# Giving the second level of the gated expert sum from VectorE to TensorE, with a shorter end of the last stage

## The chip, the cores and the metric

The kernel runs on one core of a Trainium2 chip. Its time is the device time of one execution, in microseconds. Before the change it is 437.8 us, the median of 3 runs (437.61 to 437.95).

## What is computed

The input is x with 32 sequences of 128 positions and 128 features, all in f32, and a context of the same shape. There are two gated residual blocks:

```
x = x + tanh(g_xattn) * attention16(layernorm(x), ctx, ctx)
x = x + tanh(g_ffn)   * block(layernorm(x))

def block(x):
    attn_out = causal_attention16(rope(x), rope(x), x) @ out_proj
    x1    = layernorm(x + attn_out) * ln1_w + ln1_b
    gates = softmax(x1 @ gate_w.T + gate_b)            # 8 experts
    top_gates, top = top_k(gates, 2)
    y[e]  = x1 @ expert_w[e].T + expert_b[e]           # all 8 are computed
    moe   = sum over the two chosen experts of top_gates * y[e]
    return layernorm(x1 + moe) * ln2_w + ln2_b
```

## The kernel before

Two sequences form a pair (g, 0 to 15; `LAST` is 15, `G` is 2). The first three quarters of the time are the two attentions, in slots of one tile. What this case is about is the last phase, which turns each pair's attention output into the result. It begins in the last attention slots (the `early` functions) and then runs in bodies s = 3, 4, ... (`z_steps`), one for each pair. Every engine has its own program, written out by hand, and its order is the order of the code: an engine that waits for a semaphore holds up all behind it. A body works on several pairs at once, in stages that are one body apart.

TensorE, body s, in this order: the second four experts of pair s-2 (`experts(..., 1)`, L927), transposes of pair s's attention output (L878), the product of the gates with the expert biases of pair s-3 (L946), the transpose of the gates of pair s-2 (L936), transposes of the normalised rows of pair s-1 (L901), `gated_sum` of pair s-3 (L951), the output projection of pair s (L890), the gate logits of pair s-1 (L913), and the first four experts of pair s-1 (`experts(..., 0)`, L927). An f32 product is two instructions, each with its weight load.

The four experts of the first half (in `s_bank`) are weighted and added up by VectorE from PSUM: eight instructions `z_acc` (L1232), four experts for two sequences. The four of the second half (in `st_bank`) are weighted by ScalarE into the tile `z_gated` (L1070; for the last pair L1081). VectorE adds these four to two (`gated_pairs`, L1241, 128x512) and the two to one (`gated_sum`, L1248, 128x256, tile `z_gated_sum`). TensorE multiplies the result by the identity matrix `idf`, so that it is accumulated in PSUM on the gated biases; one VectorE addition (`experts_add`, L1258) then joins it with `z_acc`. For pair 15 there are no VectorE levels: TensorE sums the four weighted experts by four identity products (`last_gated_sum`, L959), and then adds the biases (L962).

VectorE, body s: `gated_pairs` of pair s-3; the negated mean of pair s-4; `gating` of pair s-2 (L1203 to L1217: top two, sum, reciprocal, gates), with `gated_sum` of pair s-3 inside it; the accumulations of pair s-2; the attention addition of pair s (L1145, which waits for the projection); `experts_add` of pair s-3 (L1258); statistics and moments of both (L1152, L1158, L1266, L1272).

The first experts of a pair are not begun before all eight accumulations of the pair ahead have read the same banks (`pe.wait_ge(z_acc, g * ACC)`).

In the last two bodies there is no new pair. At the very end VectorE has additions, statistics and moments of pairs 14 and 15, then `weigh` (L1289) for both and `close` (L1298) for both. The factor 1/sqrt(var + eps) is made by GpSimd in two instructions (L796 and the power, L798), for pair 14 and then for pair 15; each `close` waits for its own. ScalarE issues the two last stores (L1131).

Of the kernel before, what the change touches and what calls it, by code (L numbers as in the profile page):

```python
# [53 lines left out]
def gated_block_kernel(nc, x, ctx_in, g_x, g_f, wq_t, wk_t, wv_t, wo_t, bq, bk, bv, bo,  # L54
# [3 lines left out]
    with es:  # L58
# [736 lines left out]
        def rstd_of(pool, v_in, v_eps, r_out, semaphore, k):  # L795
            pool.tensor_scalar(v_eps, v_in, 1.0, EPS, ALU.mult, ALU.add).then_inc(semaphore, 1)  # L796
            pool.wait_ge(semaphore, k + 1)
            pool.tensor_tensor(r_out, v_eps, mhalf[:, :], ALU.pow).then_inc(semaphore, 1)  # L798
# [14 lines left out]
        zst2 = two("z_stats2_", [P, G, 6]); zmv2 = two("z_mv2_", [P, G, 2]); zve2 = two("z_ve2_", [P, G])  # L813
        zrs2 = two("z_rstd2_", [P, G]); znb2 = two("z_offset2_", [P, G]); zy = two("z_y2", [P, G, P]); zyw = sb("z_yw", [P, G, P]); zyc = two("z_yc", [P, G, P])
        zsum = two("z_x1_moe", [P, G, P]); zyg = sb("z_gated", [P, G, HALF, P]); zyp = sb("z_gated_pairs", [P, G, HALF // 2, P]); zyq = sb("z_gated_sum", [P, G, P]); zo = [sb(f"z_o{i}", [P, G, P]) for i in range(4)]
# [6 lines left out]
        z_gtc = sem("z_gates_t_copied"); z_y = [sem(f"z_experts{k}") for k in range(2)]; z_yg = sem("z_experts_gated"); z_yp = sem("z_gated_pairs_summed"); z_yq = sem("z_gated_summed"); z_yb = sem("z_expert_bias")  # L822
# [43 lines left out]
        def z_pe(pe):  # L866
# [50 lines left out]
            def experts(g, gc, k):  # L917
                i = gc % 2
                if gc == 0:
                    pe.wait_ge(ex, LAST_TILE if k else LAST_TILE - 2)  # L920
                if gc >= 1:
                    if k == 0:
                        pe.wait_ge(z_acc, g * ACC)
                for b in range(G):
                    if gc >= 1 and k == 1:
                        pe.wait_ge(z_yg, (g - 1) * G + b + 1)
                    ins = pe.matmul(e_bank[b][k][:, :], zx1t[i][:, b * P:(b + 1) * P],  # L927
                                    ewt[:, k * 512:(k + 1) * 512], start=True, stop=True)
                ins.then_inc(z_y[k], 1)
# [18 lines left out]
            def gated_sum(g, gc):  # L948
                dst = u_bank[1][:, 0:W]
                pe.wait_ge(z_yq, g + 1)  # L950
                pe.matmul(dst.rearrange("q (b d) -> q b d", b=G), idf[:, :], zyq[:, :, :],  # L951
                          start=False, stop=True).then_inc(z_yb, 1)

            def last_gated_sum(g, gc):
                dst = t_bank[:, 0:W]
                pe.wait_ge(z_x1c, GROUPS)
                for e in range(HALF):
                    pe.wait_ge(z_yg, g * G + e + 1)
                    pe.matmul(dst.rearrange("q (b d) -> q b d", b=G), idf[:, :], zyg[:, :, e, :],  # L959
                              start=e == 0, stop=False)  # L960
                pe.wait_ge(z_gtc, g + 1)
                pe.matmul(dst, zgt[gc % 2][:, :], ebs[:, :], start=False, stop=True).then_inc(z_yb, 1)  # L962
# [54 lines left out]
        def z_act(act):  # L1017
# [56 lines left out]
            def gate_last_experts(g, gc):  # L1074
                i = gc % 2
                act.wait_ge(z_gate, (g + 1) * GATE)
                act.wait_ge(z_y[1], g + 1)
                act.wait_ge(z_yp, g)
                for e in range(HALF):
                    for b in range(G):  # L1080
                        ins = act.activation(zyg[:, b, e, :], e_bank[b][1][:, e * P:(e + 1) * P], ACT.Copy,  # L1081
                                             scale=zg[i][:, b, HALF + e:HALF + e + 1])
                    ins.then_inc(z_yg, 1)
# [54 lines left out]
        def z_dve(dve):  # L1138
# [57 lines left out]
            def gating(g, gc, second_level=None):  # L1196
# [15 lines left out]
                if second_level is not None:  # L1212
                    gated_sum(*second_level)
# [6 lines left out]
            def experts(g, gc):  # L1220
                i = gc % 2
                k = g * ACC
                dve.wait_ge(z_x1, (g + 1) * 2)
                dve.wait_ge(z_gate, (g + 1) * GATE)
                dve.wait_ge(z_y[0], g + 1)
                if gc >= 2:
                    dve.wait_ge(z_all, (g - 2) * ALL + 1)
                for e in range(HALF):
                    for b in range(G):
                        if e >= 1:  # L1230
                            dve.wait_ge(z_acc, k + (e - 1) * G + b + 1)
                        dve.scalar_tensor_tensor(  # L1232
                            out=zacc[i][e % 2][:, b, :], in0=e_bank[b][0][:, e * P:(e + 1) * P],
                            scalar=zg[i][:, b, e:e + 1], in1=zacc[i][(e + 1) % 2][:, b, :] if e else zx1[i][:, b, :],
                            op0=ALU.mult, op1=ALU.add).then_inc(z_acc, 1)

            def gated_pairs(g, gc):
                dve.wait_ge(z_yg, (g + 1) * G)
                if gc >= 1:
                    dve.wait_ge(z_yq, g)  # L1240
                dve.tensor_tensor(zyp[:, :, :, :], zyg[:, :, 0:HALF // 2, :], zyg[:, :, HALF // 2:HALF, :],  # L1241
                                  ALU.add).then_inc(z_yp, 1)

            def gated_sum(g, gc):
                dve.wait_ge(z_yp, g + 1)
                if gc >= 1:
                    dve.wait_ge(z_yb, g)
                dve.tensor_tensor(zyq[:, :, :], zyp[:, :, 0, :], zyp[:, :, 1, :], ALU.add).then_inc(z_yq, 1)  # L1248

            def experts_add(g, gc):  # L1250
# [6 lines left out]
                dve.wait_ge(z_acc, (g + 1) * ACC)  # L1257
# [21 lines left out]
            def all_experts(g, gc):  # L1279
                experts_add(g, gc)  # L1280
                experts_stats(g, gc)
                experts_moments(g, gc)
                experts_minus_mean(g, gc)

# [7 lines left out]
            def close(g):  # L1292
                i = g % 2
                dve.wait_ge(z_rs2, (LAST - 1) * 3 + (i + 1) * 2)
# [6 lines left out]
            def body(s, c):  # L1301
                if in_z(c, 2) and s - 2 < LAST:
# [4 lines left out]
                    gating(s - 2, c - 2, (s - 3, c - 3) if in_z(c, 3) else None)  # L1307
                if s - 2 == LAST:
                    gating(s - 2, c - 2)
                    gated_pairs(s - 3, c - 3)  # L1310
                    gated_sum(s - 3, c - 3)
# [12 lines left out]
                else:  # L1324
                    if s - 1 == LAST:
                        shift_logits(s - 1, c - 1)
                    if s - 3 == LAST - 2:
                        all_experts(s - 3, c - 3)
# [31 lines left out]
        def z_pool(pool):  # L1360
# [203 lines left out]
```

## Time and profile before

| | |
|---|---|
| median of 3 runs | 437.8 us |
| the profiled execution, its own time | 437.07 us |
| its span, first to last instruction | 435.3 us |
| TensorE matmul busy in the span | 383.0 us (88%) |
| VectorE busy | 368.9 us (85%) |
| ScalarE busy | 288.6 us (66%) |
| GpSimd busy | 314.9 us (72%) |
| granted TensorE clock, mean | 0.994 |

The profile is of one execution. Times in it count from the first instruction. PE is TensorE's matmuls, PEld its weight loads, DVE VectorE, ACT ScalarE, POOL GpSimd. A timeline row joins neighbours of one line: its length runs from the first start to the last end. A matmul's end is modelled, and two that follow each other overlap in the rows, so their distance is read from start to start.

### The profile page before, as it was taken

How to read it: one execution, taken by the hardware profiler on the slowest of the kernel's cores; microseconds unless marked ns; L12 is line 12 of the kernel's file. 1: busy time of each engine (PE TensorE's matmuls, PEld its weight loads, DVE VectorE, ACT ScalarE, POOL GpSimd, SP SyncE). 2: the span in 40 equal slices, each digit the busy share in tenths (PEclk: the TensorE clock that was granted, in tenths of full speed). 3: DMA queues.
4: the chain of work that ended last, by engine and by line, in shares of the span. 5: the costliest groups of instructions: out<-in, count | busy, mean ns of one | idle time of the engine just before them, and what ended most of it. 6: DMA issues, size and time to landing. Idle time of an engine off the chain costs nothing.

```text
span 435.3 us, 17717 instructions
## 1 busy us (share of the span) xinstructions
PE 383.0 (88%) x6538; PEld 232.0 (53%) x6538; DVE 368.9 (85%) x1218; ACT 288.6 (66%) x728; POOL 314.9 (72%) x712
## 2 busy tenths in 40 slices
PE   0368888898888899999999999999999999999993
PEld 0134544454444556666666666666664655555542
DVE  6588999999998787788888788778867999999996
ACT  1126767767776666666666666667774888888872
POOL 4456757766778988888888888885241478778774
PEclk9999999999999999999999999999999999999997
DMA  6855686585554333344334344344000000000001
GB/s 163 195 158 159 175 206 166 154 186 150 130 150 110 103 100 100 99 107 112 102 102 109 102 119 119 105 110 113 12 8 1 2 14 25 25 27 13 25 26 49
DMA packets 88037, 42.76 MB, mean 98 GB/s; under 512 B 16000, under 2 KB 87824, under 8 KB 87952
## 3 DMA queue, kind: packets, MB, share of 16 engines
q1 hardware_dynamic: 80864, 39.59, 34.4%
q10 hardware_dynamic: 7088, 2.04, 2.0%
q8 instruction: 53, 0.87, 0.9%
q14 instruction: 32, 0.26, 0.2%
HBM read 5.69 MB, written 2.10 MB: 18 GB/s over the span
## 4 chain that ended last, share of the span: by engine, by line
PE 29%; DVE 21%; issue 4%; ACT 2%; POOL 1%; POOLq 0%; DVEq 0%; ACTq 0%
PE u_bank L499 7%; DVE z_acc L1232 5%; PE s_bank L421 5%; PE s_bank L434 4%; DVE r L697 2%; PE t_bank L413 2%; DVE z_gated_pairs L1241 2%; PE t_bank L407 2%; PE u_bank L514 1%; DVE z_stats L1266 1%; ACT part L577 1%; PE s_bank L927 1%; DVE z_stats L1152 1%; DVE z_h L1145 1%; PE st_bank L927 1%
## 5 line engine op out<-in xcount | busy, mean ns | idle before, releaser
L716 DVE TENSOR_REDUCE nm<-s_bank 128x4 f32<-128x512 f32 x256 | 171.5, 682 | 35.9 <-PE s_bank L434 33.6
L599 ACT ACTIVATE pt<-st_bank 128x512 f32<-128x512 f32 x250 | 147.5, 602 | 73.8 <-PE st_bank L434 51.4
L434 PE MATMUL s_bank<-qk 64*64 64x128 bf16 (+1 forms) x1584 | 103.7, 220 | 12.0 <-DVE nm L716 5.5
L499 PE MATMUL u_bank<-pt,vaug 128*32 128x128 f32 x2048 | 108.2, 286 | 1.7
L434 PE MATMUL st_bank<-qk 64*64 64x128 bf16 (+1 forms) x1540 | 98.3, 218 | 0.1
L434 PEld LDWEIGHTS s_bank<-qk 64*64 64x64 bf16 (+1 forms) x1584 | 73.8, 104 | 35.9 <-issue 18.7
L434 PEld LDWEIGHTS st_bank<-qk 64*64 64x64 bf16 (+1 forms) x1540 | 69.2, 103 | 0.3 <-issue 0.3
L499 PEld LDWEIGHTS u_bank<-pt,vaug 128*32 128x32 f32 x2048 | 41.2, 108 | 27.5 <-issue 5.2
L421 PE MATMUL s_bank<-mqk,idb 64*64 64x256 bf16 x256 | 38.3, 292 | 0.5 <-ACT pt L599 0.4
L327 POOL TENSOR_TENSOR part<-r,part 128x512 bf16<-128x512 f32 x32 | 37.1, 1158 | 1.4
L421 PE MATMUL st_bank<-mkq,idb 64*64 64x256 bf16 x244 | 35.7, 293 | 0.0
L606 ACT ACTIVATE mts<-m_bank 128x128 bf16<-128x128 bf16 x63 | 17.5, 278 | 24.5 <-PE m_bank L509 24.5
L338 POOL TENSOR_SCALAR mst<-nm 128x16 bf16<-128x16 f32 x64 | 13.1, 205 | 27.7 <-DVE nm L716 27.7
L927 PE MATMUL s_bank<-ewt,z_x_t 128*128 128x512 f32 x64 | 31.7, 618 | 1.0 <-DVE z_acc L1232 0.4
L514 PE MATMUL u_bank<-idf,us 128*128 128x128 f32 x128 | 28.0, 300 | 5.2 <-ACT us L615 4.9
L1070 ACT ACTIVATE z_gated<-st_bank,z_gates 128x128 f32<-128x128 f32 x120 | 32.4, 382 | 0.0
L927 PE MATMUL st_bank<-ewt,z_x_t 128*128 128x512 f32 x64 | 30.2, 594 | 0.0
L322 POOL TENSOR_SCALAR part<-r 128x512 bf16<-128x512 f32 x32 | 19.8, 617 | 10.8 <-DVE r L692 6.3
L421 PEld LDWEIGHTS s_bank<-mqk,idb 64*64 64x64 bf16 x256 | 14.4, 103 | 24.3 <-issue 14.0
L796 POOL TENSOR_SCALAR z_ve<-z_mv 128x2 f32<-128x2 f32 x32 | 6.4, 201 | 28.3 <-DVE z_mv L1158 25.5
L1232 DVE SCALAR_TENSOR_TENSOR z_acc<-s_bank,z_gates,z_acc 128x128 f32<-128x128 f32 x96 | 26.1, 342 | 0.0
L280 POOL TENSOR_TENSOR rstd<-ve,mhalf 128x2 f32<-128x2 f32 x32 | 22.6, 708 | 2.7
(138 smaller groups left out, 826.3 us busy)
## 6 DMA issues: line engine op xcount, KB each, us to landing
qk<-part SPq DMA_DIRECT2D x221, 128.0 KB, 2.7
x_all<-x SPq DMA_DIRECT2D x16, 128.0 KB, 2.7
qk<-qrow SPq DMA_DIRECT2D x32, 64.0 KB, 2.2
c_all<-ctx_in SPq DMA_DIRECT2D x14, 128.0 KB, 2.8
out<-z_o SPq DMA_DIRECT2D x14, 128.0 KB, 1.8
qk<-mts ACTq DMA_DIRECT2D x34, 32.0 KB, 2.7
qk<-mts SPq DMA_DIRECT2D x30, 32.0 KB, 2.1
ewt<-exp_t SPq DMA_DIRECT2D x1, 512.0 KB
```

Source lines behind the costliest of these rows:

```text
L280: pool.tensor_tensor(rstd[u % 2][:, :], ve[u % 2][:, :], mhalf[:, :], ALU.pow).then_inc(rstd_s, 1)
L322: pool.tensor_scalar(part[u % 2][:, 1:2 * PARTS:PARTS, :], r32[:, :].rearrange("c (o t) -> c o t", o=2), 1.0, 0.0, ALU.mult, ALU.add).then ...
L327: pool.tensor_tensor(part[u % 2][:, 2:2 * PARTS:PARTS, :], r32[:, :].rearrange("c (o t) -> c o t", o=2), part[u % 2][:, 1:2 * PARTS:PARTS, ...
L421: pe.matmul(to, idb[rows, rows], mask[rows, rows].unsqueeze(1).broadcast_to([64, HEADS, 64]), start=True, stop=False, skip_group_check=True)
L434: ins = pe.matmul(to[outs, :], fixed[:, outs], moving, start=not masked, stop=True, skip_group_check=masked)
L499: ins = pe.matmul(u_bank[b][32 * j:32 * j + 32, r * P:(r + 1) * P], v, pt[m % 4][:, j, :], start=half == 0, stop=half == 1, skip_group_che ...
L514: ins = pe.transpose(u_bank[q % 2][:, W + r * P:W + (r + 1) * P], us[q % 2][:, r * P:(r + 1) * P], idf[:, :])
L599: act.activation(pt[m % 4][:, :, :].rearrange("k j q -> k (j q)"), transposed_bank(m)[:, :], ACT.Exp).then_inc(ex, 1)
L716: dve.tensor_reduce(nm[q % 2][:, first:first + HEADS], s_bank[n % 2][:, :].rearrange("q (j k) -> q j k", j=HEADS), AX_X, ALU.max, negate=T ...
L927: ins = pe.matmul(e_bank[b][k][:, :], zx1t[i][:, b * P:(b + 1) * P], ewt[:, k * 512:(k + 1) * 512], start=True, stop=True)
L1070: ins = act.activation(zyg[:, b, e, :], e_bank[b][1][:, e * P:(e + 1) * P], ACT.Copy, scale=zg[i][:, b, HALF + e:HALF + e + 1])
L1232: dve.scalar_tensor_tensor(out=zacc[i][e % 2][:, b, :], in0=e_bank[b][0][:, e * P:(e + 1) * P], scalar=zg[i][:, b, e:e + 1], in1=zacc[i][( ...
```

## The change

The second level of the gated sum leaves VectorE. TensorE takes the two halves of `z_gated_pairs` with two identity products, both accumulated on the biases. `gated_pairs` now waits for that product (`z_yb`), since it is what frees its tile.

The wait in front of the first experts is split by sequence: the products of sequence b wait for the accumulation of sequence b alone.

For pair 15, ScalarE weights two of the second four experts and TensorE sums these two. VectorE accumulates the other two itself, straight from PSUM, after ScalarE has read the bank; it has twelve accumulations in that body and no longer eight.

The moments of pair 13 move into the gating of pair 15, and their negated mean behind it. The factors of pairs 14 and 15 are made together, by one pair of GpSimd instructions over 128x4, and both `close` wait for them.

```diff
-        def rstd_of(pool, v_in, v_eps, r_out, semaphore, k):
+        def rstd_of(pool, v_in, v_eps, r_out, semaphore, k, power=mhalf[:, :]):
             pool.tensor_scalar(v_eps, v_in, 1.0, EPS, ALU.mult, ALU.add).then_inc(semaphore, 1)
             pool.wait_ge(semaphore, k + 1)
-            pool.tensor_tensor(r_out, v_eps, mhalf[:, :], ALU.pow).then_inc(semaphore, 1)
+            pool.tensor_tensor(r_out, v_eps, power, ALU.pow).then_inc(semaphore, 1)
...
-                if gc >= 1:
-                    if k == 0:
-                        pe.wait_ge(z_acc, g * ACC)
-                for b in range(G):
+                for b in range(G):
+                    if gc >= 1 and k == 0:
+                        pe.wait_ge(z_acc, g * ACC - G + b + 1)
...
             def gated_sum(g, gc):
                 dst = u_bank[1][:, 0:W]
-                pe.wait_ge(z_yq, g + 1)
-                pe.matmul(dst.rearrange("q (b d) -> q b d", b=G), idf[:, :], zyq[:, :, :],
-                          start=False, stop=True).then_inc(z_yb, 1)
+                pe.wait_ge(z_yp, g + 1)
+                for e in range(HALF // 2):
+                    ins = pe.matmul(dst.rearrange("q (b d) -> q b d", b=G), idf[:, :], zyp[:, :, e, :],
+                                    start=False, stop=e == HALF // 2 - 1)
+                ins.then_inc(z_yb, 1)
 
             def last_gated_sum(g, gc):
                 dst = t_bank[:, 0:W]
                 pe.wait_ge(z_x1c, GROUPS)
-                for e in range(HALF):
+                for e in range(HALF // 2):
                     pe.wait_ge(z_yg, g * G + e + 1)
                     pe.matmul(dst.rearrange("q (b d) -> q b d", b=G), idf[:, :], zyg[:, :, e, :],
                               start=e == 0, stop=False)
...
                 act.wait_ge(z_yp, g)
-                for e in range(HALF):
+                for e in range(HALF // 2):
...
-                if second_level is not None:
-                    gated_sum(*second_level)
+                if g == LAST:
+                    experts_moments(LAST - 2, gc - 2)
...
-                for e in range(HALF):
+                for e in range(HALF if g < LAST else HALF + HALF // 2):
+                    half, col, gate = (0, e, e) if e < HALF else (1, e - HALF // 2, e + HALF // 2)
+                    if e == HALF:
+                        dve.wait_ge(z_y[1], g + 1)
+                        dve.wait_ge(z_yg, (g + 1) * G)
                     for b in range(G):
                         if e >= 1:
                             dve.wait_ge(z_acc, k + (e - 1) * G + b + 1)
                         dve.scalar_tensor_tensor(
-                            out=zacc[i][e % 2][:, b, :], in0=e_bank[b][0][:, e * P:(e + 1) * P],
-                            scalar=zg[i][:, b, e:e + 1], in1=zacc[i][(e + 1) % 2][:, b, :] if e else zx1[i][:, b, :],
+                            out=zacc[i][e % 2][:, b, :], in0=e_bank[b][half][:, col * P:(col + 1) * P],
+                            scalar=zg[i][:, b, gate:gate + 1], in1=zacc[i][(e + 1) % 2][:, b, :] if e else zx1[i][:, b, :],
                             op0=ALU.mult, op1=ALU.add).then_inc(z_acc, 1)
...
             def gated_pairs(g, gc):
                 dve.wait_ge(z_yg, (g + 1) * G)
                 if gc >= 1:
-                    dve.wait_ge(z_yq, g)
+                    dve.wait_ge(z_yb, g)
                 dve.tensor_tensor(zyp[:, :, :, :], zyg[:, :, 0:HALF // 2, :], zyg[:, :, HALF // 2:HALF, :],
                                   ALU.add).then_inc(z_yp, 1)
-
-            def gated_sum(g, gc):
-                dve.wait_ge(z_yp, g + 1)
-                if gc >= 1:
-                    dve.wait_ge(z_yb, g)
-                dve.tensor_tensor(zyq[:, :, :], zyp[:, :, 0, :], zyp[:, :, 1, :], ALU.add).then_inc(z_yq, 1)
...
-                dve.wait_ge(z_acc, (g + 1) * ACC)
+                dve.wait_ge(z_acc, (g + 1) * ACC + (G * HALF // 2 if g == LAST else 0))
...
-                dve.wait_ge(z_rs2, (LAST - 1) * 3 + (i + 1) * 2)
+                dve.wait_ge(z_rs2, (LAST - 1) * 3 + 2)
...
                 if s - 2 == LAST:
                     gating(s - 2, c - 2)
+                    experts_minus_mean(s - 4, c - 4)
                     gated_pairs(s - 3, c - 3)
-                    gated_sum(s - 3, c - 3)
...
-                        all_experts(s - 3, c - 3)
+                        experts_add(s - 3, c - 3)
+                        experts_stats(s - 3, c - 3)
...
             def factor2(g, gc):
                 i = g % 2
                 pool.wait_ge(z_all, moments_done(g))
-                k = g * 3 if g < LAST else (LAST - 1) * 3 + 2
+                k = g * 3
                 rstd_of(pool, zmv2[i][:, :, 1], zve2[i][:, :], zrs2[i][:, :], z_rs2, k)
-                if g < LAST - 1:
-                    pool.wait_ge(z_rs2, k + 2)
-                    pool.wait_ge(z_all, (g + 1) * ALL)
-                    pool.tensor_tensor(znb2[i][:, :], zmn2[i][:, :], zrs2[i][:, :], ALU.mult).then_inc(z_rs2, 1)
+                pool.wait_ge(z_rs2, k + 2)
+                pool.wait_ge(z_all, (g + 1) * ALL)
+                pool.tensor_tensor(znb2[i][:, :], zmn2[i][:, :], zrs2[i][:, :], ALU.mult).then_inc(z_rs2, 1)
+
+            def last_factors():
+                pool.wait_ge(z_all, moments_done(LAST))
+                rstd_of(pool, zmv2_both[:, :, :, 1], zve2_both[:, :, :], zrs2_both[:, :, :], z_rs2, (LAST - 1) * 3,
+                        mhalf[:, :].unsqueeze(1).broadcast_to([P, 2, G]))
 
             def body(s, c):
                 if in_z(c, 1):
                     x1(s - 1, c - 1)
                 if s - 3 == LAST:
-                    factor2(s - 4, c - 4)
-                    factor2(s - 3, c - 3)
+                    last_factors()
```

## Rows read from the trace of the kernel before

**Rows 1.** Last phase by window: length, busy PE, PEld, DVE, ACT, POOL, clock, DMA.

```profile
338.87:420.87 82.00, 80.62 (x322) 46.49 (x321) 80.17 (x456) 69.01 (x220) 63.27 (x128) 1.00 0.06 19
```

**Rows 2.** Chain of waits in one step, 376.4 to 382.8: its shares by line.

```profile
by line: DVE z_acc L1232 28.1%; DVE z_h L1145 12.9%; issue 10.1%; DVE z_gated_pairs L1241 9.0%; DVE z_stats L1266 6.2%; DVE z_stats L1152 6.1%; DVE z_x_moe L1258 5.2%; DVE z_gated_sum L1248 5.2%; DVE z_others L1211 4.5%; DVE z_mv L1158 3.3%
```

**Rows 3.** TensorE's timeline, first full body: start, length, line, operation, tiles, count.

```profile
332.79 1.96 PE L927 MATMUL s_bank<-ewt,z_x_t 128*128 128x512 f32 x4
...
337.58 0.60 PE L951 MATMUL u_bank<-z_gated_sum,idf 128*128 128x256 f32 x2
338.01 0.61 PE L890 MATMUL m_bank<-wo,z_att_t 128*128 128x128 f32 x4
338.46 0.55 PE L913 MATMUL u_bank<-gwt,z_x_t 128*128 128x8 f32 x4
338.87 1.96 PE L927 MATMUL s_bank<-ewt,z_x_t 128*128 128x512 f32 x4
```

**Rows 4.** TensorE's timeline, a later body.

```profile
376.55 1.98 PE L927 MATMUL s_bank<-ewt,z_x_t 128*128 128x512 f32 x4
...
382.23 0.56 PE L913 MATMUL u_bank<-gwt,z_x_t 128*128 128x8 f32 x4
382.84 1.98 PE L927 MATMUL s_bank<-ewt,z_x_t 128*128 128x512 f32 x4
```

**Rows 5.** VectorE's timeline of the same step, and one row of the next.

```profile
376.41 0.41 DVE L1145 TENSOR_TENSOR z_h<-m_bank,xn_all 128x256 f32<-128x256 f32 x1
...
379.81 0.41 DVE L1248 TENSOR_TENSOR z_gated_sum<-z_gated_pairs 128x256 f32<-128x256 f32 x1
380.14 0.17 DVE L1215 TENSOR_TENSOR z_top<-z_exps,z_others 128x16 f32<-128x16 f32 x1
380.34 0.19 DVE L1217 TENSOR_TENSOR z_gates<-z_top,z_rsum 128x16 f32<-128x16 f32 x1
...
385.03 0.69 DVE L1241 TENSOR_TENSOR z_gated_pairs<-z_gated 128x512 f32<-128x512 f32 x1 [0.18 <-issue]
```

**Rows 6.** TensorE's timeline, last bodies.

```profile
414.58 1.98 PE L927 MATMUL s_bank<-ewt,z_x_t 128*128 128x512 f32 x4
...
418.62 0.28 PE L936 MATMUL u_bank<-idf,z_gates 128*16 128x128 f32 x1 [0.34 <-DVE z_gates L1217]
...
420.22 0.51 PE L913 MATMUL u_bank<-gwt,z_x_t 128*128 128x8 f32 x4
420.87 1.98 PE L927 MATMUL s_bank<-ewt,z_x_t 128*128 128x512 f32 x4
...
425.67 1.91 PE L959 MATMUL t_bank<-z_gated,idf 128*128 128x256 f32 x8
427.51 0.69 PE L962 MATMUL t_bank<-ebs,z_gates_t 16*128 16x256 f32 x2
```

**Rows 7.** VectorE's timeline, end; in brackets idle before and who ended it.

```profile
424.25 0.83 DVE L1248 TENSOR_TENSOR z_gated_sum<-z_gated_pairs 128x256 f32<-128x256 f32 x1
425.00 0.59 DVE L1232 SCALAR_TENSOR_TENSOR z_acc<-s_bank,z_gates,z_x 128x128 f32<-128x128 f32 x2
...
428.24 0.42 DVE L1258 TENSOR_TENSOR z_x_moe<-t_bank,z_acc 128x256 f32<-128x256 f32 x1 [0.76 <-PE t_bank L962]
...
432.31 0.61 DVE L1298 SCALAR_TENSOR_TENSOR z_o<-z_yc,z_rstd,x_all 128x128 f32<-128x128 f32 x2 [0.59 <-POOL z_rstd L798]
```

**Rows 8.** ScalarE's timeline, end.

```profile
424.66 2.17 ACT L1081 ACTIVATE z_gated<-st_bank,z_gates 128x128 f32<-128x128 f32 x8 [1.20 <-PE st_bank L927]
```

**Rows 9.** GpSimd's timeline, end.

```profile
423.45 0.22 POOL L1410 TENSOR_TENSOR z_offset<-z_minus_mean,z_rstd 128x2 f32<-128x2 f32 x1
...
429.94 0.35 POOL L796 TENSOR_SCALAR z_ve<-z_mv 128x2 f32<-128x2 f32 x1 [0.66 <-DVE z_mv L1272]
430.37 0.70 POOL L798 TENSOR_TENSOR z_rstd<-z_ve,mhalf 128x2 f32<-128x2 f32 x1
431.16 0.35 POOL L796 TENSOR_SCALAR z_ve<-z_mv 128x2 f32<-128x2 f32 x1
```

More of the change, by code:

```diff
@@ L812, in gated_block_kernel @@
         zacc = [[sb(f"z_acc{i}{j}", [P, G, P]) for j in range(2)] for i in range(2)]
-        zst2 = two("z_stats2_", [P, G, 6]); zmv2 = two("z_mv2_", [P, G, 2]); zve2 = two("z_ve2_", [P, G])
-        zrs2 = two("z_rstd2_", [P, G]); znb2 = two("z_offset2_", [P, G]); zy = two("z_y2", [P, G, P]); zyw = sb("z_yw", [P, G, P]); zyc = two("z_yc", [P, G, P])
-        zsum = two("z_x1_moe", [P, G, P]); zyg = sb("z_gated", [P, G, HALF, P]); zyp = sb("z_gated_pairs", [P, G, HALF // 2, P]); zyq = sb("z_gated_sum", [P, G, P]); zo = [sb(f"z_o{i}", [P, G, P]) for i in range(4)]
+        zst2 = two("z_stats2_", [P, G, 6]); zmv2_both = sb("z_mv2", [P, 2, G, 2]); zve2_both = sb("z_ve2", [P, 2, G])
+        zrs2_both = sb("z_rstd2", [P, 2, G]); zmv2, zve2, zrs2 = ([t[:, i] for i in range(2)] for t in (zmv2_both, zve2_both, zrs2_both)); znb2 = two("z_offset2_", [P, G]); zy = two("z_y2", [P, G, P]); zyw = sb("z_yw", [P, G, P]); zyc = two("z_yc", [P, G, P])
+        zsum = two("z_x1_moe", [P, G, P]); zyg = sb("z_gated", [P, G, HALF, P]); zyp = sb("z_gated_pairs", [P, G, HALF // 2, P]); zo = [sb(f"z_o{i}", [P, G, P]) for i in range(4)]
         z_ot = sem("z_att_transposed"); z_otc = sem("z_att_t_copied")
@@ L821, in gated_block_kernel @@
         z_gate = sem("z_gate_steps"); z_exp = sem("z_gate_exp"); z_gt = sem("z_gates_transposed")
-        z_gtc = sem("z_gates_t_copied"); z_y = [sem(f"z_experts{k}") for k in range(2)]; z_yg = sem("z_experts_gated"); z_yp = sem("z_gated_pairs_summed"); z_yq = sem("z_gated_summed"); z_yb = sem("z_expert_bias")
+        z_gtc = sem("z_gates_t_copied"); z_y = [sem(f"z_experts{k}") for k in range(2)]; z_yg = sem("z_experts_gated"); z_yp = sem("z_gated_pairs_summed"); z_yb = sem("z_expert_bias")
         z_acc = sem("z_accumulated"); z_all = sem("z_all_summed_steps"); z_rs2 = sem("z_rstd2_steps"); z_y2s = sem("z_normalised2")
@@ L1194, in shift_logits, with gating @@
                 logit_maxima(g, gc)
-            def gating(g, gc, second_level=None):
+            def gating(g, gc):
                 i = gc % 2
@@ L1276, in experts_minus_mean @@
                 dve.tensor_scalar(zmn2[g % 2][:, :], zmv2[g % 2][:, :, 0], -1.0, 0.0, ALU.mult, ALU.add).then_inc(z_all, 1)
[L1279 to L1283, printed above, removed]
             def weigh(g):
@@ L1306, in body @@
                         experts_minus_mean(s - 4, c - 4)
-                    gating(s - 2, c - 2, (s - 3, c - 3) if in_z(c, 3) else None)
+                    gating(s - 2, c - 2)
                 if s - 2 == LAST:
                     gating(s - 2, c - 2)
+                    experts_minus_mean(s - 4, c - 4)
                     gated_pairs(s - 3, c - 3)
-                    gated_sum(s - 3, c - 3)
                 if in_z(c, 2):
```

## The prediction

> **What bounds the kernel now.** I read the page first. Its shares over the whole span tell nothing of a 0.4 us edit, and it says that matmul ends are modelled, so a busy TensorE need not be a full one. The edit acts in the last phase (16 pairs of sequences through projection, gating and experts). The stretch 338.87 to 420.87 has VectorE at 80.17 of 82.00 us, and TensorE at 80.62 [rows 1]. So next the chain of waits inside one step, 376.4 to 382.8: its largest entries are VectorE's, and TensorE is not among them [rows 2]. VectorE sets the pace: 6.29 us a step.
>
> The question of this case is how far TensorE is behind, because it is to receive what VectorE gives up. Its timeline answers that, if one reads starts and not ends. In the first body, from 332.79 to 338.87, nothing in it waits: the last group before the experts, the logits, starts at 338.46 and the experts 0.41 later. That is 6.07 us of work, start to start (6.08 by the rounded rows) [rows 3]. In a later body the same two starts are 382.23 and 382.84, 0.61 apart: 0.20 us of idle time in front of the experts, where TensorE waits for VectorE's last accumulation; the step is 376.55 to 382.84, 6.29 us [rows 4]. Every other start in the body has the same distance as in the free body. **TensorE therefore has 0.22 us of room in a 6.29 us step**, no more.
>
> **The change, part by part.**
>
> *The second level of the gated sum.* VectorE loses one 128x256 addition: it starts at 379.81 and the next instruction at 380.14, so 0.33 us a step; VectorE alone would then go at 6.29 - 0.33 = 5.96 us [rows 5]. TensorE gets one more f32 product of 256 columns, two instructions. The existing product starts at 337.58 and the projection behind it at 338.01: 0.43 us for two [rows 3]. In the closing sum eight such instructions, which read the same kind of strided view, take 425.67 to 427.51, 0.22 us each and 0.1 at the end [rows 6]. So 0.43 us, in the middle of the body, with nothing beside it on TensorE. Bounds: 0.43 from these rows, 0.64 if each were spaced as the 0.32 us that stands at a 16-row product (from 427.51, the pair in 0.69) [rows 6]; below, nothing if it hid itself wholly. I take 0.43, since both groups of the very form show it.
>
> The new step is the larger of VectorE's 5.96 and TensorE's 6.07 + 0.43 = 6.50. **The bound changes engine, and the step grows by 0.21 us.** The cover for the product was 0.22 us and its price is 0.43.
>
> I checked that the loop through both engines does not add a wait. VectorE restarts on the projection of a step; from its start at 376.41 it now takes to 380.53 for the gates [rows 5], 4.1 us, without the addition 3.8. TensorE wants these gates 4.6 us or more after the projection, so 0.6 us is left (an estimate from the rows). The accumulations end early by the same token. The per-sequence wait in front of the experts (first expert product after seven of eight accumulations) would give 0.26 us back where TensorE waits, and nothing here, because after the change it does not wait there. ScalarE's work hangs on TensorE's transposes and has 0.43 us more room before the logits. The pair addition now waits for the previous product on TensorE, done over 2 us earlier: nothing. The 0.3 us that one step loses today (idle before 385.03, a step of 6.59) lies on VectorE and would be hidden [rows 5].
>
> There are 13 such bodies from 332.79. The pair-14 experts start today at 414.58 [rows 6]. After: 332.79 + 13 x 6.506 = 417.37. **Term 1: +2.79 us.**
>
> *The last full body* (no projection in it). Expert products fill 3.51 us from 417.37, to 420.89; VectorE has the gates at about 420.94, so the gate transpose is at 420.99. From it to the logits is 418.62 to 420.22, 1.60 us, plus 0.43; then the logits' four instructions 0.36 without a wait (today 0.65, 420.22 to 420.87) [rows 6]. Sum: 420.99 + 2.03 + 0.36 = 423.38 for the last experts against 420.87. **Term 1 and this together: +2.51 us.**
>
> *The end of the last stage.* ScalarE gates two experts of each sequence instead of four, TensorE sums two products instead of four (four instructions fewer, 4 x 0.216 = -0.86), but the step before carries its extra product (+0.43), and 0.02 goes where the experts no longer wait. VectorE does four more accumulations from PSUM. Which is last? TensorE: today from 420.87 to the closing addition at 428.24 is 7.37 us [rows 6, 7]; after, 7.37 - 0.86 + 0.43 - 0.02 = 6.92, so 430.30. VectorE: the logits end at 423.53; it reaches its first accumulation about 3.0 us later (today 4.27, less 0.75 for the addition at 424.25 and 0.5 for the moments and the negated mean that were moved behind or into gaps), at 426.6, then twelve accumulations at 0.26 and one addition 0.33: 430.0 [rows 7]. ScalarE: last expert products end at 427.06, four activations 1.2 us (eight take 2.17 [rows 8]): 428.3. TensorE is last by 0.3 us. **The closing addition is at 430.29, +2.05 us.**
>
> *Combined rstd.* Today two pairs of GpSimd instructions in a row: the first power starts at 430.37, the second pair at 431.16, and VectorE's last two outputs wait for it until 432.31 [rows 7, 9]. Now one pair over four columns: it waits for all four moments (+0.13), and the outputs follow the one power, four in a row at 0.27. With P for the power's duration, the last output ends 4.69 us after the closing addition's start today (432.93 less 428.24). After: 1.83 to the pair's start (1.70 today, from 429.94, and the 0.13), 0.43 to the power, P, 0.04 to VectorE, 0.80 to the fourth output's start and 0.35 for it, 3.45 + P. No row has a power over four columns. Lower bound: 0.70, as over two [rows 9]. Upper: a product over two columns takes 0.22 [rows 9], so 0.48 may be the power itself, twice for four columns: 1.2. I take the middle, 0.95: -0.29 (-0.54 to -0.04). The two stores then start 0.5 us apart, not 1.2 (before, the 432.31 less the 431.11 at which the first power of 0.70 let the first output go), so the second may land late by some 0.1 us, an estimate.
>
> *Moved moments of pair 13, GpSimd's order.* Its factor comes some 3 us later, in front of the store work of pair 12, which then ends before the factors of the last pairs are wanted, by 0.4 us: nothing. Without that cover it would cost what it is late.
>
> **Sum:** +2.05 - 0.29 + 0.1 = **+1.86 us** on the profiled 437.07 us (span 435.3): 438.93. The timed runs have their median 0.73 above it, so 437.8 + 1.86 = **439.7 us**, 0.4% slower.
>
> A rule speaks against this. The stretch shows weight loads busy 46.49 of 82.00 us [rows 1]. The Trainium skill ("Perfetto Trace Analysis", section Identifying the Most-Contended Engine) tells one to judge TensorE's headroom by weight-load share and not by matmul share. By it TensorE at 57% has room and VectorE at 98% is the engine to unload, and the step would fall below 6.29 (first rival). The free body's 6.07 us disagrees: a TensorE at 57% by that measure is full, since f32 products take 0.43 us for 0.19 us of load.
>
> **The rivals.**
>
> *The product is hidden (faster).* Place: between the transposes and the projection; it decides if its cost on TensorE is under 0.22 us a body. If it were nothing, the step would be 6.07, 13 x 0.22 = 2.9 us less to pair 14 (with the hidden 0.3), 0.3 in the last body, 0.9 in the closing sum, 0.3 in the tail: -4.4, 433.4 us. For it: the chain names VectorE [rows 2]. Against: starts on TensorE are rigid to 0.01 us over the bodies, and the very form costs 0.43. 8%.
>
> *Half of it is covered.* If it costs just the idle 0.22, the step stays 6.29, and the end alone counts: -0.65 on TensorE, -0.29 and +0.1 in the tail: 437.0 us. For it: loads overlap other groups. Against: at 0.22 us an instruction the load of 0.19 us is already hidden in all rows. 8%.
>
> *A further wait in the new regime (slower still).* With TensorE as pace maker a late ScalarE or VectorE result within its body costs 1:1, 13 times: 0.1 us each is 1.3 us, 441.0 us, more with a power of 1.2 us. For it: the gates' margin is only 0.6 us and the gated experts' similar. Against: all of them gain room with a longer step. 8%.
>
> **How the numbers follow.** Forecast 76%, rivals 8% each. Forecast alone: 439.1 to 440.2 (power, stores, some tenths for the pace). The range that leaves 2 in 10 out reaches down to the half-covered case and up into the last: 437.4 to 441.0. What this kernel can tell from no change is about 0.2%, 0.9 us. Faster by more than that: the first rival and half of the second, 12%. Within: the other half, and 6% for an end that gives more than I grant, 10%. Slower 78%.
>
> **What would show it.** In the profile after: starts of the first expert product 6.50 us apart with 0.41 us between logits and experts in every body; VectorE idle some 0.5 us a step, before the attention addition, ended by the projection; chain of waits through TensorE from 338 on. The closing sum with four instructions, the last addition waiting for TensorE; one power before four outputs in a row. The forecast is wrong if the distance is 6.3 or less, or if four product instructions take under 0.65 us.

## The result, and the profile after

The changed kernel takes 438.52 us (median of 16 runs, 437.98 to 438.98), the kernel before 437.26 us (16 runs, 436.60 to 437.95, the three of above among them). The ratio is 1.0029, 95% interval 1.0022 to 1.0036: slower by 1.26 us. The forecast was slower by 1.86 us; the stated range, 437.4 to 441.0 us, holds the result. The profiled execution's span grew from 435.3 to 436.8 us.

| | before | after |
|---|---|---|
| span | 435.3 us | 436.8 us |
| TensorE matmul busy | 383.0 us | 386.0 us |
| VectorE busy | 368.9 us | 366.3 us |
| step, from first experts to first experts (13 to pair 14, mean) | 6.29 us | 6.46 us |
| first experts of pair 14 | 414.58 | 416.96 |
| closing addition | 428.24 | 430.06 |
| end of the last output | 432.93 | 434.40 |

The last phase by window, over twelve steps (length, busy PE, PEld, DVE, ACT, POOL, clock, DMA). It answers to [rows 1]: TensorE is at 77.53 of 77.53 us, and VectorE, which stood at 98%, is at 72.00, 93%.

```profile
339.43:416.96 77.53, 77.53 (x326) 46.80 (x326) 72.00 (x409) 63.63 (x204) 58.13 (x118) 1.00 0.06 18
```

The chain of waits in one step, by line, against [rows 2]. There is nothing but TensorE in it.

```profile
by line: PE s_bank L926 28.0%; PE st_bank L926 26.4%; PE u_bank L951 13.3%; PE u_bank L945 9.6%; PE m_bank L890 8.6%; PE u_bank L913 5.3%; PE t_bank L901 3.4%; PE t_bank L878 3.4%; PE u_bank L935 3.2%
```

TensorE's timeline of one step, against [rows 3, 4]. The first experts start at 365.27 and 371.73, 6.46 us apart. Logits and experts are 0.36 us apart (371.37 and 371.73), without idle time; the prediction had 0.41. The second-level products are four instructions, from 370.06 to the projection at 370.92: 0.86 us, where two took 0.43.

```profile
365.27 1.96 PE L926 MATMUL s_bank<-ewt,z_x_t 128*128 128x512 f32 x4
...
368.79 0.38 PE L878 MATMUL t_bank<-idf,c_all 128*128 128x128 f32 x2
369.10 0.69 PE L945 MATMUL u_bank<-ebs,z_gates_t 16*128 16x256 f32 x2
369.72 0.28 PE L935 MATMUL u_bank<-idf,z_gates 128*16 128x128 f32 x1
369.84 0.38 PE L901 MATMUL t_bank<-idf,z_n 128*128 128x128 f32 x2
370.06 1.03 PE L951 MATMUL u_bank<-z_gated_pairs,idf 128*128 128x256 f32 x4
370.92 0.61 PE L890 MATMUL m_bank<-wo,z_att_t 128*128 128x128 f32 x4
371.37 0.51 PE L913 MATMUL u_bank<-gwt,z_x_t 128*128 128x8 f32 x4
371.73 0.68 PE L926 MATMUL s_bank<-ewt,z_x_t 128*128 128x512 f32 x1
```

VectorE's timeline of the same step, against [rows 5]. It idles 0.30 us for the projection before the attention addition, where some 0.5 us had been forecast. The attention addition starts at 365.11 and the last gate instruction ends at 369.01, 3.90 us, where it was 4.12 (376.41 to 380.53 in [rows 5]). The 128x256 addition is gone, but the one behind it now starts 0.18 us after the last replace (368.45 to 368.63).

```profile
365.11 0.43 DVE L1146 TENSOR_TENSOR z_h<-m_bank,xn_all 128x256 f32<-128x256 f32 x1 [0.30 <-PE m_bank L890]
...
368.31 0.15 DVE L1212 MATCH_REPLACE8 z_others<-z_sorted,z_exps 128x8 f32<-128x8 f32 x1
368.38 0.08 DVE L1212 MATCH_VALUE_LOAD z_others<-z_sorted,z_exps 128x8 f32 x1
368.45 0.15 DVE L1212 MATCH_REPLACE8 z_others<-z_sorted,z_exps 128x8 f32<-128x8 f32 x1
368.63 0.18 DVE L1216 TENSOR_TENSOR z_top<-z_exps,z_others 128x16 f32<-128x16 f32 x1
368.84 0.17 DVE L1218 TENSOR_TENSOR z_gates<-z_top,z_rsum 128x16 f32<-128x16 f32 x1
...
371.57 0.42 DVE L1146 TENSOR_TENSOR z_h<-m_bank,xn_all 128x256 f32<-128x256 f32 x1 [0.30 <-PE m_bank L890]
```

The end, TensorE, against [rows 6]: the closing sum is four instructions.

```profile
423.16 1.96 PE L926 MATMUL s_bank<-ewt,z_x_t 128*128 128x512 f32 x4
...
428.37 1.03 PE L960 MATMUL t_bank<-z_gated,idf 128*128 128x256 f32 x4
429.33 0.69 PE L963 MATMUL t_bank<-ebs,z_gates_t 16*128 16x256 f32 x2
```

The end, VectorE, against [rows 7]: the closing addition still waits for TensorE, now 0.23 us, and the four last outputs follow each other after one wait.

```profile
429.43 0.41 DVE L1257 TENSOR_TENSOR z_x_moe<-u_bank,z_acc 128x256 f32<-128x256 f32 x1
430.06 0.42 DVE L1257 TENSOR_TENSOR z_x_moe<-t_bank,z_acc 128x256 f32<-128x256 f32 x1 [0.23 <-PE t_bank L963]
...
433.26 1.14 DVE L1291 SCALAR_TENSOR_TENSOR z_o<-z_yc,z_rstd,x_all 128x128 f32<-128x128 f32 x4 [0.41 <-POOL z_rstd L798]
```

The end, GpSimd, against [rows 9]: one power over 128x4, of 1.02 us.

```profile
431.90 0.23 POOL L796 TENSOR_SCALAR z_ve<-z_mv 128x4 f32<-128x4 f32 x1 [1.34 <-DVE z_mv L1271]
432.20 1.02 POOL L798 TENSOR_TENSOR z_rstd<-z_ve,mhalf 128x4 f32<-128x4 f32 x1
```

### The profile page after: what moved, and what is told of

Read it like the earlier page. It is cut to its first block, busy times and chain, and to the rows that moved or that the text cites. A ratio compares the mean times of both kernels' runs of the same rounds, so it can differ in the third digit from the quotient of the medians.

```text
span 436.8 us, 17739 instructions
## 1 busy us (share of the span) xinstructions
PE 386.0 (88%) x6564; PEld 235.8 (54%) x6564; DVE 366.3 (84%) x1207; ACT 287.7 (66%) x724; POOL 314.2 (72%) x710
## 4 chain that ended last, share of the span: by engine, by line
PE 47%; DVE 5%; issue 3%; ACT 2%; POOL 1%; POOLq 0%; DVEq 0%; ACTq 0%
PE u_bank L499 7%; PE s_bank L926 6%; PE st_bank L926 6%; PE s_bank L421 4%; PE s_bank L434 4%; PE u_bank L951 3%; DVE r L697 2%; PE u_bank L945 2%; PE t_bank L413 2%; PE t_bank L407 2%; PE m_bank L890 2%; PE u_bank L514 1%; ACT part L577 1%; PE t_bank L408 1%; PE u_bank L913 1%
## 5 line engine op out<-in xcount | busy, mean ns | idle before, releaser
L796 POOL TENSOR_SCALAR z_ve<-z_mv 128x2 f32<-128x2 f32 (+1 forms) x31 | 6.0, 192 | 32.0 <-DVE z_mv L1159 27.9
```

## The experiments

All were timed beside the kernel before, each with 5 to 11 runs; ratios are to it, since its median moved between 437.2 and 437.7 us. "Step" is the distance of the first experts in the trace. The differences here are all under 1%; an interval that holds 1 shows no difference.

### Each half of the change by itself

**end_only**: the changed kernel with the second level back on VectorE for pairs 0 to 13. The cut shows TensorE's side; VectorE's addition stands in its old place again.

```diff
+        BY_PE = {14}
...
+                if g not in BY_PE:
+                    pe.wait_ge(z_yq, sums_by_dve(g + 1))
+                    pe.matmul(dst..., idf[:, :], zyq[:, :, :], start=False, stop=True).then_inc(z_yb, 1)
+                    return
```

> The changed kernel with the second level given back to VectorE for pairs 0 to 13 (pair 14 stays with TensorE); the new end of the last stage stays. My theory (TensorE is the pace maker of the changed kernel, and only because of the added product): the step returns to 6.29 us, VectorE's; the first experts of the last pair start about 0.3 us earlier than before by the split wait; the closing sum is four instructions shorter and carries one product more; one power less at the end. Together 1.0 us less than before: 436.2 us, ratio 0.9977. Rival (the new end costs, or gives nothing, and the product is not the whole loss): 437.3 us or more.

Measured: 436.26 us, ratio 0.9978 (0.9969 to 0.9986). TensorE's timeline shows the step of before, 364.17 to 370.46, and the idle time before the experts (0.61 from 369.85). The total is as expected, but not every part of it: the experts of pair 15 start 87.93 us after those of pair 1, where it was 88.08: 0.15 us earlier and not 0.3. The closing addition (6.93 us after them and not 7.37) and the last output give the rest.

```profile
364.17 1.98 PE L933 MATMUL s_bank<-ewt,z_x_t 128*128 128x512 f32 x4
...
369.85 0.55 PE L920 MATMUL u_bank<-gwt,z_x_t 128*128 128x8 f32 x4
370.46 1.98 PE L933 MATMUL s_bank<-ewt,z_x_t 128*128 128x512 f32 x4
```

**second_only**: the kernel before, and only the second level moved. The cut shows TensorE's side; VectorE's addition is taken out.

```diff
-                pe.wait_ge(z_yq, g + 1)
-                pe.matmul(dst..., idf[:, :], zyq[:, :, :], start=False, stop=True).then_inc(z_yb, 1)
+                pe.wait_ge(z_yp, g + 1)
+                for e in range(HALF // 2):
+                    ins = pe.matmul(dst..., idf[:, :], zyp[:, :, e, :], start=False, stop=e == HALF // 2 - 1)
+                ins.then_inc(z_yb, 1)
```

> The kernel before with the second level on TensorE in all pairs and nothing else of the change. My theory: steps of 6.46 us, 13 of them, 2.2 us more than before by the last body, 0.4 more in the last sum, nothing back at the end: +2.5 us, 439.8 us, ratio 1.0057. Rival (gains and losses of the step cancel, and the loss lies in the new end): as before, 437.3.

Measured: 439.63 us, ratio 1.0054 (1.0042 to 1.0066), all 13 steps 6.46. So the moved sum costs 0.54% and the new end gives back 0.22%; the two make 0.32%, the whole change 0.29%.

### The price of the product

**one_product**: the changed kernel with one identity product for pairs 0 to 13. It leaves the other half of the second-level sum out of its result; it is there for its time alone.

```diff
-                for e in range(HALF // 2):
+                for e in range(1 if g < LAST - 1 else 2):
```

> The changed kernel, but for pairs 0 to 13 TensorE multiplies only the first half of the pair sums (one product, not two; the second half is left out of the result). VectorE is unloaded as in the change. This is what the change would be if its product cost TensorE nothing. My theory (price of the product 0.43 us a step, 1:1): steps of 6.07 us, with the logits again 0.04 us late by ScalarE's copy (a 0.07 us distance inside the logits, 0.03 in the changed kernel), 13 x 0.39 and 0.4 in the last body: 5.3 us under the changed kernel, 433.2 us. Rival (another wait, on VectorE or ScalarE, holds the step at 6.29 once the product is gone): 436.2 us.

Measured: 433.52 us, ratio 0.9913 (0.9900 to 0.9925). The step is 6.07 (363.57 to 369.64), the logits are 0.55 long again and 0.41 ahead of the experts, where the changed kernel has 0.51 and 0.36.

```profile
363.57 1.96 PE L926 MATMUL s_bank<-ewt,z_x_t 128*128 128x512 f32 x4
...
368.35 0.60 PE L951 MATMUL u_bank<-z_gated_pairs,idf 128*128 128x256 f32 x2
...
369.23 0.55 PE L913 MATMUL u_bank<-gwt,z_x_t 128*128 128x8 f32 x4
369.64 1.53 PE L926 MATMUL s_bank<-ewt,z_x_t 128*128 128x512 f32 x3
```

The product costs 0.39 us a step: its 0.43, less 0.04 that the logits had waited. This is the kernel that the first rival describes: had the product been free, the change would have been 0.87% faster. VectorE does not wait in these steps either, but for one place that the last section names: its attention additions are 6.07 apart, so both engines are at their limit here.

**both_sum**: the changed kernel, and VectorE does the removed addition as well.

```diff
+                if second_level is not None:
+                    gated_sum(*second_level)      # result not read
```

> The changed kernel, and VectorE makes its old 128x256 second-level addition as well in every step, in its old place, with a result that nobody reads. My theory (VectorE has 0.5 us of idle time a step in the changed kernel, TensorE none): steps stay 6.46, 438.5 us, the same as the changed kernel, at most 0.3 more from the last two steps. Rival (VectorE is still on the path, its gates or accumulations are waited for): 0.33 us a step, 4 us more, 442.5 us.

Measured: 439.00 us, ratio 1.0030 (1.0018 to 1.0041), as the changed kernel (1.0029). Steps 6.46. VectorE's timeline: the addition stands at 367.94 and the step goes from 364.53 to 371.00; the work fits into the idle time. Behind these 13 steps it does not: the body of pair 14, which has no projection, takes 6.43 us (416.39 to 422.82) and not 6.20. VectorE is on the path there, for 0.23 us, too little for the times to show.

```profile
364.53 0.42 DVE L1158 TENSOR_TENSOR z_h<-m_bank,xn_all 128x256 f32<-128x256 f32 x1
...
367.87 0.15 DVE L1224 MATCH_REPLACE8 z_others<-z_sorted,z_exps 128x8 f32<-128x8 f32 x1
367.94 0.42 DVE L1266 TENSOR_TENSOR z_gated_sum<-z_gated_pairs 128x256 f32<-128x256 f32 x1
368.27 0.17 DVE L1230 TENSOR_TENSOR z_top<-z_exps,z_others 128x16 f32<-128x16 f32 x1
...
371.00 0.42 DVE L1158 TENSOR_TENSOR z_h<-m_bank,xn_all 128x256 f32<-128x256 f32 x1
```

**whole_wait**: the changed kernel with the unsplit wait before the first experts.

```diff
-                for b in range(G):
-                    if gc >= 1 and k == 0:
-                        pe.wait_ge(z_acc, g * ACC - G + b + 1)
+                if gc >= 1 and k == 0:
+                    pe.wait_ge(z_acc, g * ACC)
+                for b in range(G):
```

> The changed kernel with the old wait in front of the first experts (all eight accumulations for both sequences). My theory (TensorE never waits there in the changed kernel, VectorE's last accumulation starts 0.7 us before): no change, 438.5 us, steps of 6.46. Rival (the split wait is what keeps the step at 6.46): up to 0.26 us a step, 3.4 us more.

Measured: 438.84 us, ratio 1.0028 (1.0016 to 1.0039), steps 6.46 and the last body 6.20. The split wait gives nothing here.

**rstd_only**: the kernel before with `last_factors` alone.

> The kernel before with the one edit that the factors of pairs 14 and 15 are made by one pair of GpSimd instructions over 128x4. My theory: the power over four columns takes 1.02 us (0.70 over two, as in the changed kernel's trace), and the last output ends 0.35 us earlier: 436.8 us, ratio 0.9992. Rival (the two stores, now 0.5 us apart, delay each other, or the power costs as much as two): 437.2 us, no change.

Measured: 437.29 us, ratio 0.9999 (0.9990 to 1.0008). The times can't tell 0.35 us from nothing (the interval is 0.4 us to either side). In the trace the last output ends 4.33 us after the start of the closing addition (429.01 to 433.35), before it was 4.69, in the changed kernel 4.33.

### Lending TensorE back some time

**mix3**: the changed kernel with the second level on TensorE for every third pair only (`BY_PE = {2, 5, 8, 11, 14}`), on VectorE for the others.

> The changed kernel with the second level on TensorE only for pairs 2, 5, 8, 11 and 14, on VectorE for the others. My theory: both engines have room to lend over neighbouring steps (0.6 us): TensorE's mean step is (2 x 6.07 + 6.46) / 3 = 6.20, VectorE's (2 x 6.29 + 5.96) / 3 = 6.18, so 6.20 instead of 6.29 over 13 steps, 1.2 us less than the kernel with the new end alone: 435.0 us. Rival (the steps are coupled too tightly, each pays its own slower engine): two steps at 6.29 and one at 6.46, mean 6.35, 437.0 us.

Measured: 435.66 us, ratio 0.9965 (0.9952 to 0.9978). Steps 6.48, 6.07, 6.25 in turn, mean 6.27. This lies between the two theories: the step after a TensorE step is short, the next one waits 0.18 us for VectorE.

**full_rows**: the changed kernel with the 16-row product padded to 128 rows.

```diff
-        ... ebs = sb("ebs", [G * NE, W])
+        ... ebs = sb("ebs", [P, W])
...
-        ... zgt = two("z_gates_t", [G * NE, P])
+        ... zgt = two("z_gates_t", [P, P])
...
+            for t in zgt:
+                dve.memset(t[:, :], 0.0).then_inc(c_two, 1)
...
-                act.activation(zgt[i][:, :], u_bank[0][0:G * NE, W:W + P], ACT.Copy).then_inc(z_gtc, 1)
+                act.activation(zgt[i][0:G * NE, :], u_bank[0][0:G * NE, W:W + P], ACT.Copy).then_inc(z_gtc, 1)
```

> The changed kernel, but the product of gates and expert biases has its 16 rows padded with zero rows to 128 (tiles z_gates_t and ebs of 128 partitions, cleared once at the start). My theory (TensorE's stream sets the step, and the 0.20 + 0.32 + 0.31 us around the 16-row product are weight loads that are not taken ahead): the three distances become 0.11 + 0.22 + 0.22, the step 6.46 - 0.28 = 6.18 us, 13 steps and the last two bodies: 4.3 us less than the changed kernel, 434.2 us. Rival 1 (the distances come from something else than the 16 rows): 438.5 us. Rival 2 (another engine takes over at once, at the 6.29 of before): 436.2 us.

Measured: 437.10 us, ratio 0.9990 (0.9981 to 0.9998), steps 6.39. None of the three expected times came: the theory had 6.18 us a step. TensorE's timeline:

```profile
368.68 0.38 PE L882 MATMUL t_bank<-idf,c_all 128*128 128x128 f32 x2
368.90 0.60 PE L949 MATMUL u_bank<-ebs,z_gates_t 128*128 128x256 f32 x2
369.34 0.27 PE L939 MATMUL u_bank<-idf,z_gates 128*16 128x128 f32 x1
369.63 0.41 PE L905 MATMUL t_bank<-idf,z_n 128*128 128x128 f32 x2
369.88 1.03 PE L955 MATMUL u_bank<-z_gated_pairs,idf 128*128 128x256 f32 x4
```

The distances are as expected: the padded product starts 0.22 after the attention transposes (368.68 to 368.90; in the changed kernel 368.79 to 369.10, 0.31), the gate transpose 0.44 after it (there 369.10 to 369.72, 0.62), so 0.27 us is gone. But the transposes of the normalised rows start 0.29 later instead of 0.12 (369.72 to 369.84). Most of the gain had turned into a new wait. The profile names no releaser for it. In the code TensorE waits there for ScalarE's copy of the attention transposes out of the same bank; that copy ended at 369.49, and the first weight load of the transposes came at 369.60. That it is this wait is argued from these two times; no run isolates it.

**full_order**: full_rows, with one of the two products in front of these transposes.

```diff
+                if early_half:
+                    gated_sum(s - 3, c - 3, (0,))
                 if in_z(c, 1) and s - 1 < LAST:
                     transpose_n(s - 1, c - 1)
                 if in_z(c, 3) and s - 3 < LAST:
-                    gated_sum(s - 3, c - 3)
+                    gated_sum(s - 3, c - 3, (1,) if early_half else (0, 1))
```

> The padded kernel, and one of the two identity products goes in front of the transposes of the normalised rows, the other stays behind them. The padded kernel's steps were 6.39 and not 6.18: its transposes start 0.295 and 0.138 us after what is ahead of them, where 0.113 and 0.109 stood. My theory (they now wait for ScalarE's copy of the attention transposes out of the same bank): 0.43 us of product covers that 0.21 us; the logits are then late by 0.04, as with one product. Steps of 6.22, 2.1 us under the padded kernel: 435.0 us. Rival (the wait is for something that itself follows TensorE's order, the gates): steps stay at 6.39, 437.1 us.

Measured: 435.05 us, ratio 0.9940 (0.9926 to 0.9954), steps 6.22, as expected; the rival, a wait for the gates, is out. A product now fills the wait, and the transposes start 0.44 after it began, as for any product:

```profile
368.73 0.27 PE L939 MATMUL u_bank<-idf,z_gates 128*16 128x128 f32 x1
368.84 0.60 PE L955 MATMUL u_bank<-z_gated_pairs,idf 128*128 128x256 f32 x2
369.28 0.38 PE L905 MATMUL t_bank<-idf,z_n 128*128 128x128 f32 x2
369.50 0.60 PE L955 MATMUL u_bank<-z_gated_pairs,idf 128*128 128x256 f32 x2
```

**full_mix2** is full_rows with `BY_PE` of the odd pairs and 14 (second level on TensorE for these, on VectorE for the others), **full_order_mix2** is full_order with the same set.

> The padded kernel with the second level on TensorE only for odd pairs and pair 14. My theory: steps with it 6.18 (TensorE), steps without it 5.96 (TensorE alone 5.79, but it waits for VectorE's seventh accumulation), mean 6.07: 1.3 us less than the padded kernel, 432.9 us. Rival (VectorE's 6.29 counts in each step that has its addition): mean 6.23, 0.7 us more than the padded kernel, 434.9 us.

Measured: 434.58 us, ratio 0.9934 (0.9921 to 0.9948). Of the kernels that do the whole of the reference's work, this one, full_order and the next one are the fastest, and level within the intervals. Steps 6.02 and 6.41, mean 6.22, where I had 6.07: I had again left out the wait of the transposes (6.41 and not 6.18).

> The same order, with the second level on TensorE only for odd pairs and pair 14. My theory: steps 6.22 with it and 6.02 without, mean 6.12 (6.21 in the mixed kernel with the old order): 1.2 us less, 433.4 us. Rival (VectorE, at 6.29 and 5.96, mean 6.13, cannot follow the 6.12 and adds waits): 434.0 us or more.

Measured: 434.89 us, ratio 0.9937 (0.9925 to 0.9949), where I had 433.4. Steps 6.13 and 6.24, mean 6.19: the rival is right, VectorE holds it. Its attention additions in a step without and one with the addition:

```profile
364.33 0.42 DVE L1170 TENSOR_TENSOR z_h<-m_bank,xn_all 128x256 f32<-128x256 f32 x1
...
370.39 0.41 DVE L1170 TENSOR_TENSOR z_h<-m_bank,xn_all 128x256 f32<-128x256 f32 x1
...
376.69 0.42 DVE L1170 TENSOR_TENSOR z_h<-m_bank,xn_all 128x256 f32<-128x256 f32 x1
```

They are 6.06 apart across the step without it and 6.30 across the step with it. The trace shows no wait of VectorE between 345 and 410, so its own step without the addition is 6.06 us, not the 5.96 that I had used everywhere.

## Why the prediction was right, and where its size was off

*The bound changes engine, the step grows.* Right, and shown from three sides: the chain and the windows of the changed kernel; second_only, in which this part alone gives steps of 6.46; and one_product and both_sum, where taking work from TensorE shortens the step and giving work to VectorE doesn't lengthen it. The first rival and the half-covered one are out: the price was 0.39, above the 0.22 of cover. The third, a further wait, is out for the 13 steps, in which TensorE has no idle time; the last body has one, of which more below.

*Its size: 0.17, not 0.21 us a step.* The term was 6.07 + 0.43. The free body's 6.07 us was not free: inside the logits two starts were 0.07 apart and are 0.03 now. The logits waited there for ScalarE's copy of the transposed rows, and the added product gives that copy 0.43 us more. The rows show it. Before, the copy ended at 369.54 and the first weight load of the logits started 0.05 us later:

```profile
368.98 0.56 ACT L1030 ACTIVATE z_x_t<-t_bank,l1bc,l1wc 128x256 f32<-128x256 f32 x1
369.59 0.52 PEld L913 LDWEIGHTS u_bank<-gwt,z_x_t 128*128 128x128 f32 x4
```

In the changed kernel the copy ended at 370.82 and the load started 0.44 later, ahead of its product:

```profile
370.26 0.56 ACT L1031 ACTIVATE z_x_t<-t_bank,l1bc,l1wc 128x256 f32<-128x256 f32 x1
371.26 0.53 PEld L913 LDWEIGHTS u_bank<-gwt,z_x_t 128*128 128x128 f32 x4
```

In one_product and in full_order, where one product stands behind the transposes, the load is 0.05 behind the copy again, and two starts are 0.07 or 0.08 apart. I had named that margin ("ScalarE's work has 0.43 us more room before the logits") and had taken its worth as nothing. 13 x 0.044 = 0.57 us: the first experts of pair 14 came 84.00 us after those of pair 1, not 84.58. one_product, with the old distance, has the 6.07 again.

*VectorE's 5.96 us.* Mis-sized, though nothing in the sum of the steps hung on it. The addition took 0.33 us from start to start but stood in a latency: the subtraction behind it waits for the last replace anyway. With the addition in place it starts 0.07 us after that replace (367.87 and 367.94 in both_sum); without it the subtraction starts 0.18 after it. So 0.33 + 0.07 - 0.18 = 0.22 us is what VectorE saved. It did cost in the last body: the gates came at 420.72, 3.76 us after the first experts of pair 14, where I had 3.57, and TensorE waited for them:

```profile
420.54 0.18 DVE L1218 TENSOR_TENSOR z_gates<-z_top,z_rsum 128x16 f32<-128x16 f32 x1
420.77 0.28 PE L935 MATMUL u_bank<-idf,z_gates 128*16 128x128 f32 x1
```

That body took 6.20 us instead of 6.01: +0.19. Of this, 0.11 is the difference of 0.33 and 0.22. Another 0.04 is the term above, since the experts of pair 14 now start that much sooner behind the projection; 0.04 is left without a name. The body of 6.43 in both_sum shows from the other side that VectorE's work counts there 1:1.

*The closing sum.* Right: 6.90 us from the last experts to the closing addition, 6.92 forecast, with TensorE last and VectorE 0.23 us idle in front of it. No run takes this part of the change alone; in end_only it measures 6.93.

*Combined factors.* Right within its bounds: the power took 1.02 (0.70 to 1.2, taken 0.95); the last output ended 4.33 after the addition's start (4.40 forecast), since the power started 0.30 after the instruction in front of it and not 0.43 (that instruction took 0.23 and not 0.35). The second store was not late: 2.38 us from the last output's end to the span's, 2.34 before; I had given it 0.1. That this part gives 0.35 us is read from traces, the timing doesn't resolve it.

*The sum.* From the traces: +0.17 in when the phase begins (332.96 against 332.79), +2.21 for the steps, -0.09 in the last body, -0.47 in the closing sum, -0.35 and +0.03 in the tail: +1.50, the spans' difference. The 0.17 is scatter: the first experts of pair 1 start between 332.35 and 333.64 in the traces of this case. Without it +1.33 is left, and the timed +1.26 (0.96 to 1.57) agrees. The forecast of the difference was 0.6 too high. Two errors partly cancel in that: the steps were 0.58 too long in it, the last body 0.19 too short; the tail was 0.13 better than forecast. The 439.7 us was 0.5 higher again because the three runs shown before lay above the later median (437.8, 437.3).

*The rule on TensorE's headroom.* The stretch before had weight loads busy 57%. The Trainium skill ("Perfetto Trace Analysis", section Identifying the Most-Contended Engine) has TensorE's headroom judged by that share, and by the share of peak arithmetic, instead of the matmul share. After the change the weight loads are busy 46.80 of 77.53 us, 60%, and TensorE has no idle time at all. For the f32 products of this stretch the trace decides against the weight-load share as a measure of headroom; the other measure was not taken here.

## What to carry to other kernels

Before work is moved from the pace-making engine, find one repetition in which the receiving engine did not wait, take its start-to-start time, and compare the free time with the price on that engine; a busy share says neither. Then check whether what is removed stood in the shadow of a latency, since only the rest is saved. A gain on the new bound engine may end at the next wait within the same body, and an instruction that must be done anyway is the thing to put there.

## What the runs showed of the hardware

The f32 product over 16 rows (of both operands) costs TensorE more than the same one padded with zeros to 128: 0.20 + 0.32 + 0.31 us from start to start around it against 0.11 + 0.22 + 0.22, though one of its weight loads takes 0.18 us against 0.19. Their weight loads differ in when they start; that of the changed kernel first. With 16 rows the load starts at 369.10 with its own product; padded, it starts at 368.80, 0.10 ahead of its product at 368.90.

```profile
369.10 0.29 PEld L945 LDWEIGHTS u_bank<-ebs,z_gates_t 16*128 16x128 f32 x2 [0.17 <-issue]
```

In full_rows:

```profile
368.80 0.30 PEld L949 LDWEIGHTS u_bank<-ebs,z_gates_t 128*128 128x128 f32 x2
```

The Trainium skill ("TensorE: Matmul & The Clock Gate", section LDWEIGHTS (loading the stationary operand)) says that the number of rows does not matter for the load. For the load's length the trace agrees (0.18 and 0.19 us); the distance of the products depends on the rows all the same.

GpSimd's power takes 0.69 to 0.72 us over 128x2 and 1.02 over 128x4, so, if it grows evenly, an estimate is 0.16 us for a further column and 0.38 besides. There is an exception: in every kernel with the moved moments of pair 13 the power of that pair, over 128x2, takes 1.10 to 1.18 us (1.17 at 425.80 in the changed kernel). VectorE runs its 128x512 pair addition and the first accumulations at the same time; that they are the reason was not tested. The extra half microsecond is hidden: GpSimd still idles 1.34 us for VectorE's moments before the last power.

In the kernel before, in end_only and in rstd_only one step, always the ninth after the first experts of pair 1, takes 6.6 and not 6.3 us, with VectorE idle before the pair addition and no releaser. The same step has a stop of VectorE in the changed kernel, second_only, whole_wait and one_product: it stands still for 0.44 us before its first accumulation (at 388.85 in the changed kernel). There TensorE sets the step and hides it, up to the 0.03 us that one_product shows. In both_sum a stop of 0.33 us stands at 407.77, and in full_rows, full_order and full_order_mix2 there is none. The cause stays open.
